# Zeroing the expert pages: from the SyncE queue between stack loads to the ScalarE queue at fixed steps

## What is computed

```python
q, k, v = split_heads(x @ Wq), split_heads(x @ Wk), split_heads(x @ Wv)
scores = einsum('bhqd,bhkd->bhqk', q, k) / sqrt(dh)
scores = exp(scores - max(scores, axis=-1, keepdims=True))
scores = where(mask, scores, 0.0)                  # 64 wide, around the diagonal
x1 = layernorm(x + (softmax(scores) @ v) @ Wo)
# per net: leaf = tree(x1); out = relu(x1 @ w1[leaf] + b1[leaf]) @ w2[leaf] + b2[leaf]
out = layernorm(x1 + softmax(q1 @ k1.T * scale) @ v1)
```

## Time and profile before

| what | us |
|---|---|
| runs (three) | 2205.07, 2193.43, 2202.26 |
| median | 2202.26 |
| the profiled execution, its own time | 2202.43 |
| span of its core | 2200.7 |
| PE, DVE, ACT, POOL busy in the span | 1955.7, 1599.3, 1351.9, 951.3 |
| 141 pages zeroed, first and last issue | 115.3 and 1143.8 |
| mean granted PE clock (share of full) | 0.953 |

### The profile page before, as it was taken

The page is one execution under the profiler, slowest core; times in us unless marked ns, Lnnn a source line. Parts: engine busy times, 40 slices in busy tenths (PEclk is TensorE's granted clock), DMA queues, the critical chain, the costliest instruction groups (busy, mean ns, idle before and its releaser), DMA issues. The chain is left out here.

```text
span 2200.7 us, 44841 instructions
## 1 busy us (share of the span) xinstructions
PE 1955.7 (89%) x14352; PEld 1554.8 (71%) x14352; DVE 1599.3 (73%) x4188; ACT 1351.9 (61%) x2511; POOL 951.3 (43%) x1472
## 2 busy tenths in 40 slices
PE   3979889999999999999999984687889689999997
PEld 2546567667667667677676663576878579999997
DVE  2667677787786986977977845497979367777775
ACT  1768667777777787787787732475767234444442
POOL 4313423555554565565556555300020655555511
PEclk9999999999999999999999965799999889999999
DMA  2684685767658656857765534979877333333311
GB/s 60 107 156 84 153 162 100 154 126 143 135 112 170 130 117 144 153 119 154 142 117 113 108 84 133 314 233 280 271 263 235 114 90 97 97 94 96 95 40 40
DMA packets 207298, 304.55 MB, mean 138 GB/s; under 512 B 48429, under 2 KB 108890, under 8 KB 207066
## 3 DMA queue, kind: packets, MB, share of 16 engines
q1 hardware_dynamic: 157322, 195.73, 42.8%
q0 software_dynamic: 29440, 68.98, 10.8%
q10 hardware_dynamic: 20304, 36.97, 4.5%
HBM read 104.16 MB, written 115.87 MB: 100 GB/s over the span
## 5 line engine op out<-in xcount | busy, mean ns | idle before, releaser
L1449 DVE CUSTOM_DVE_ANT_0 above<-p_half,above 128x512 f32<-128x512 f32 x1024 | 684.5, 683 | 195.0 <-ACT above L1151 140.9
L1151 ACT ACTIVATE above<-p_diff 128x512 f32<-128x512 f32 x1024 | 603.3, 605 | 215.4 <-PE p_diff L1032 185.5
L1032 PE MATMUL p_diff<-d_stack,q_stack 96*128 96x512 bf16 x1024 | 397.0, 390 | 19.1 <-DMA d_stack<-d_parts 13.9
L1036 PE MATMUL p_half<-k_stack,q_stack 96*128 96x512 bf16 x1024 | 391.3, 385 | 13.4 <-DVE row_max L1449 11.4
L1755 POOL DMA_INDIRECT raw<-sorted_y,slot x192 | 206.1, 1073 | 351.5 <-DMA sorted_y<-y_tile 296.4
L1081 PEld LDWEIGHTS p_pv<-v_win,w_win 128*128 128x128 f32 x2048 | 302.9, 197 | 46.6 <-ACT w_win L1176 6.5
L1081 PE MATMUL p_pv<-v_win,w_win 128*128 128x34 f32 x2048 | 290.4, 267 | 2.7 <-ACT w_win L1176 2.7
L205 POOL DMA_INDIRECT sorted_x<-y,slot x192 | 199.5, 1039 | 89.8 <-issue 50.3
L2002 ACT ACTIVATE pt_hi<-p_one 128x512 fp32r<-128x512 f32 x128 | 69.5, 595 | 246.3 <-PE p_one L1878 246.3
L1032 PEld LDWEIGHTS p_diff<-d_stack,q_stack 96*128 96x128 bf16 x1024 | 139.9, 138 | 74.2 <-issue 33.4
L1170 ACT ACTIVATE w_win<-p_win 128x512 f32<-128x512 f32 x256 | 154.2, 602 | 51.8 <-PE p_win L1057 46.9
(11 more groups left out here) (277 smaller groups left out, 5013.9 us busy)
## 6 DMA issues: line engine op xcount, KB each, us to landing
sorted_x<-zeros SPq DMA_DIRECT2D x141, 256.0 KB, 3.4
x_tile<-sorted_x SPq DMA_DIRECT2D x141, 256.0 KB, 4.2
sorted_y<-y_tile ACTq DMA_DIRECT2D x141, 256.0 KB, 3.8
q_stack<-q_parts SPq DMA_DIRECT2D x256, 96.0 KB, 3.6
k_stack<-k_parts SPq DMA_DIRECT2D x256, 96.0 KB, 4.1
d_stack<-d_parts SPq DMA_DIRECT2D x256, 48.0 KB, 3.5
v_win<-v_tiles POOLq DMA_DIRECT2D x16, 544.0 KB, 5.6
v_win<-v_tiles POOLq DMA_DIRECT2D x32, 272.0 KB, 6.8
```

The source lines that it names most:

```text
L1032: nc.tensor.matmul(p_diff[s % 2][:], qs, d_stack[0:SPLIT_ROWS, h, :], start=True, stop=True).then_inc(s_diff, 1)
L1036: nc.tensor.matmul(p_half[s % 3][:], qs, k_stack[0:SPLIT_ROWS, h, HALO + S // 2:HALO + S], start=True, stop=True).then_inc(s_half, 1)
L1151: nc.scalar.activation(above[:, s % 4], p_diff[s % 2][:], ACT.Relu).then_inc(s_above, 1)
L1449: nc.vector.tensor_tensor_reduce(out=above[:, s % 4], in0=p_half[s % 3][:], in1=above[:, s % 4], scale=1.0, scalar=-3.0e38, op0=ALU.add, o ...
```

## The change

The zeroing DMAs leave SP's program. ACT issues them, at the end of the steps 6, 14, ..., 62 of each unit: the pages of `clears_after(8u + h)` in step 8h + 6. Their number, size, source, target and semaphores are the same, and two per head stay two per head in units 0 to 3. The wait for the zeros tile (`s_nz`) moves to ACT's unit 0, once.

```diff
@@ SP, unit @@
                 for h in range(GH):
                     if 0 <= u + 1 < 2 * B:
                         load_stack(b, g, h)
-                    for k in clears_after(QT * u + h):
-                        clear(k // NETS, k % NETS, cleared_for(k))
@@ SP @@
-            def clear(i, n, r):
-
-                wait_alone(sp, s_nz, 6)
-                rows = xs[n][TILE * i:TILE * i + TILE, :].rearrange("(p j) c -> p (j c)", p=P)
-                sp.dma_start(rows, zeros[:]).then_inc(s_clear[r], 16)
@@ ACT @@
+            def clear(i, n, r):
+
+                rows = xs[n][TILE * i:TILE * i + TILE, :].rearrange("(p j) c -> p (j c)", p=P)
+                act.dma_start(rows, zeros[:]).then_inc(s_clear[r], 16)
+
             def unit(b, g):
                 cur = 0 <= b < B
                 u = 2 * b + g
                 if u == 0:
+                    act.wait_ge(s_nz, 6)
                     act.wait_ge(s_nt, 1)
...
                     for w, o, h in late(b, g, s, EXP2_LAG):
                         second_exponential(GH * w + h, h)
+                    if s % QT == 6:
+                        for k in clears_after(QT * u + s // QT):
+                            clear(k // NETS, k % NETS, cleared_for(k))
```

## The result

| what | before | changed |
|---|---|---|
| median, us | 2199.82 (20 runs) | 2180.16 (20 runs) |
| lowest and highest, us | 2193.43 to 2206.71 | 2173.09 to 2196.24 |
| the profiled execution, its own time and its span | 2202.43, 2200.7 | 2184.25, 2182.5 |
| ratio, with its 95% interval | 1 | 0.9918 [0.9902, 0.9935] |

The change makes the kernel 0.8% faster; 0.7% was forecast, and 2180 stands against 2187.

What follows compares the result with a forecast made beforehand. PE was taken as the bound, idling where ACT's q0 waited for SP's late last stack; gains of 18.0 us (SP) and 2.8 (clock) less 3.8 (ACT) and 2.0 (clears beside the last stack) made 15.0, so 2187 us, range 2170 to 2200.

Runs made afterwards that it cites:

- e4: The changed kernel with each clear issued as two DMAs of 64 partitions, twice the issues on ACT; 2320.26 us, ratio 1.0551.
- e2: The changed kernel with ACT's clears moved to steps 31 to 46 of each unit, behind the last stack load; 2158.35 us, ratio 0.9815.
- e1: The kernel before, with SP issuing all clears of a unit behind the stack load of its last head; 2163.82 us, ratio 0.9851.

## What to carry to other kernels

Ask first when a background transfer should run, and only then from which queue: here the stretch between two bursts of loads gave 33 us from either queue, while the new queue at the old time gave 20, and 13 on another chip. When DMA issues move to an engine that computes, one that fits under the instruction ahead of it is free and two in a row are not. When two times agree, compare them unit by unit before calling it the same cause. And when work is tied to a new engine's steps, look at the first unit, where the new place comes earlier than the old one did.

## What the runs showed of the hardware

- On ACT a DMA's issue starts together with the ACTIVATE ahead of it (306.06 for both in e4, 1398.60 for both in the earlier trace rows), or, where another ACTIVATE still runs, before it (88.54 for 88.98 in the changed kernel). The next ACTIVATE follows the issue's end by 0.1 us or a little more (88.54 + 0.81 to 89.46; 1398.60 + 0.35 to 1399.09). One issue of 0.33 us is covered by an ACTIVATE of 0.60 us: in e2 the wait for `above` is 4.5 us.
- The time to issue on ACT differs with the shape and with the place in a row. For 128 partitions of 2 KB it was 0.33 us, and 0.45 or more for the second of a pair; for 64 partitions of 2 KB (e4) 0.45 us, 0.62 for the second, and up to 2.5 us in the rows of four.
- A DMA share below 1 was no sign of free room for a second queue. Without clears beside SP's stack loads it was 0.89 in e1, at 111 GB/s; with the clears of ACT's queue the share was 0.89 again, at 154 GB/s, and the loads took 41.07 us for 33.95.
